# Cross-attention and mixture of experts on one core: key products in six banks, the maxima's scores of batch 0 ahead of most value products, normalisations and set-up transfers moved

## The reference, cut to what matters

```python
# x (8, 256, 256); ctx (8, 77, 256): 8 batches, 256 queries and 77 keys each, 16 heads of width 16
q1, q2 = heads(norm(x) @ q1_w.T), heads(norm(x) @ q2_w.T)
k1, v1 = heads(ctx @ kv1_w.T);  k2 = heads(ctx @ kv2_w.T)[keys]
attn = softmax(q1 @ k1.T / 4) - (lambda_1 - lambda_2 + 0.1) * softmax(q2 @ k2.T / 4)
x = x + rmsnorm(attn @ v1) * norm_w @ proj_w.T + proj_b
# then a mixture of 8 experts, two for each of the 2048 tokens
w, idx = top_k(softmax(norm(x) @ gate_w.T), 2);  w = w / sum(w)
x = x + sum over the two experts of w * (silu(g) * u) @ down.T,   g, u = norm(x) @ gate_up.T
```

## Time and profile before

| | |
|---|---|
| median of 3 runs | 556.19 us (552.88 to 559.12) |
| the profiled execution's own time | 557.22 us |
| its span, first to last instruction | 555.4 us |
| PE busy | 495.3 us (89%) |
| PEld busy | 363.6 us (65%) |
| VectorE busy | 386.1 us (70%) |
| ScalarE busy | 340.2 us (61%) |
| GpSimd busy | 273.4 us (49%) |
| granted TensorE clock, mean | 0.963 of full speed |
| chain that ended last | PE 67%, DVE 10%, ACT 7%, DMA 5% |

### The profile page before, as it was taken

The page is one execution under the profiler, slowest core; times in us unless marked ns, Lnnn a source line. Parts: engine busy times, 40 slices in busy tenths (PEclk is TensorE's granted clock), DMA queues, the critical chain, the costliest instruction groups (busy, mean ns, idle before and its releaser), DMA issues.

```text
span 555.4 us, 12114 instructions
## 1 busy us (share of the span) xinstructions
PE 495.3 (89%) x3741; PEld 363.6 (65%) x3756; DVE 386.1 (70%) x805; ACT 340.2 (61%) x642; POOL 273.4 (49%) x347
## 2 busy tenths in 40 slices
PE   4695889998999888799798999999999999999990
PEld 3463546775666555526566888878888888777750
DVE  5437458888888765788577997887667677666551
ACT  1220588888788888374675777766656566645530
POOL 5006464574564564203227566656567555644244
PEclk9986799999999989899999999999999999999996
DMA  7567757768658632563666777967555465554224
GB/s 215 191 171 174 239 147 231 203 171 264 192 170 253 200 118 76 179 204 112 152 137 111 158 129 195 180 120 157 94 104 86 85 84 101 96 68 77 30 30 47
DMA packets 88090, 79.89 MB, mean 144 GB/s; under 512 B 49176, under 2 KB 73368, under 8 KB 87896
## 3 DMA queue, kind: packets, MB, share of 16 engines
q1 hardware_dynamic: 76512, 63.38, 41.8%
q0 software_dynamic: 11520, 15.74, 17.6%
HBM read 49.08 MB, written 22.41 MB: 129 GB/s over the span
## 4 chain that ended last, share of the span: by engine, by line
PE 67%; DVE 10%; ACT 7%; DMA 5%; issue 5%; SPq 3%; POOL 2%; another core or an unknown queue 0%; ACTq 0%; POOLq 0%
PE bank L1459 27%; PE bank L1476 13%; PE bank L1242 5%; PE bank L1288 4%; DMA x_parts<-WE 3%; PE bank L1274 3%; PE bank L1488 2%; PE bank L1256 2%; PE bank L1311 2%; PE bank L1324 2%; DVE FB L1165 2%; PE bank L1297 2%; DVE FB L1169 2%; ACT FB L876 2%; PE bank L1336 2%
## 5 line engine op out<-in xcount | busy, mean ns | idle before, releaser
L1459 PE MATMUL bank<-FB,WE 128*128 128x0 bf16 x1440 | 187.6, 280 | 2.6 <-issue 1.0
L1459 PEld LDWEIGHTS bank<-FB,WE 128*128 x1440 | 136.1, 98 | 34.9 <-issue 4.3
L709 POOL DMA_INDIRECT out<-FB,slot_tok x60 | 99.9, 1665 | 91.2 <-DVE FB L1186 85.4
L876 ACT ACTIVATE FB<-FB 128x512 bf16<-128x512 f32 x120 | 75.6, 630 | 69.9 <-DVE FB L1165 63.8
L1169 DVE TENSOR_TENSOR FB<-FB 128x512 bf16<-128x512 f32 x120 | 83.3, 694 | 46.9 <-ACT FB L876 43.0
L1476 PE MATMUL bank<-FB,WE 128*128 128x0 bf16 x720 | 103.7, 280 | 4.3 <-DVE FB L1169 2.2
L1165 DVE TENSOR_TENSOR FB<-FB,bank 128x512 f32<-128x512 f32 x120 | 81.9, 683 | 27.8 <-ACT FB L870 21.5
L700 POOL DMA_INDIRECT FB<-x_parts,slot_tok x60 | 61.7, 1028 | 68.0 <-DMA FB<-FB 26.7
L870 ACT ACTIVATE FB<-bank 128x512 f32<-128x512 f32 x120 | 70.7, 589 | 33.9 <-PE bank L1459 29.3
L1476 PEld LDWEIGHTS bank<-FB,WE 128*128 x720 | 67.6, 98 | 23.5 <-issue 7.8
L633 POOL TENSOR_TENSOR WE<-FB,WE 128x256 bf16<-128x256 f32 x104 | 67.8, 678 | 22.1 <-ACT WE L740 22.0
(11 more groups left out here) (180 smaller groups left out, 616.4 us busy)
## 6 DMA issues: line engine op xcount, KB each, us to landing
FB<-w SPq DMA_DIRECT2D x26, 512.0 KB, 5.5
WE<-w SPq DMA_DIRECT2D x44, 256.0 KB
WE<-q_parts SPq DMA_DIRECT2D x32, 200.0 KB
WE<-x SPq DMA_DIRECT2D x16, 256.0 KB, 5.2
q_parts<-FB SPq DMA_DIRECT2D x32, 128.0 KB
x_parts<-WE SPq DMA_DIRECT2D x20, 128.0 KB, 4.0
out<-WE SPq DMA_DIRECT2D x20, 128.0 KB, 5.5
q_parts<-WE SPq DMA_DIRECT2D x16, 128.0 KB
```

Source lines behind the costliest of these rows:

```text
L709: pool.indirect_dma_start(out=out, out_offset=bass.IndirectOffsetOnAxis(ap=slot_tok[:, c:c + 1].bitcast(U32), axis=0), in_=result_tile(c), ...
L876: nc.scalar.activation(hT[k % 3][:, 0, :], hid[k % 2], ACT.Copy).then_inc(hi_ready, 1)
L1459: ins = nc.tensor.matmul(to, wf[:, bass.ds(at + o, P)], xgT[s % 2][:, 2 * part + kc, :].shape_from_register(long[s % 2]), start=(z == 0), ...
```

## The change

The keys of group m go to banks 2(m mod 3) and 2(m mod 3) + 1, so banks 0 to 5 hold them and group 3 reuses banks 0 and 1 after the first remainder. Values use banks 2 to 5 in turn. On PE the order becomes: keys, queries of batch 0, transpose of x of batch 1, values 0 and 1, queries of batch 1, scores groups 0 to 11 with values 2 to 5 after groups 1, 3, 5, 7 and the transpose of x of batch 2 after group 7; values 6 and 7 come after queries (1) of batch 2. VectorE's value copies move along, its statistics and norm of batch 1 go between the key remainders, the scaling of the projection weights comes before the values, the statistics of batch 2 between the two query remainders of batch 1 and its norm after the second maximum. On SyncE two of the eight pad transfers go between the keys' transfers, and the load of x of batch 2 goes ahead of the query transfers of batch 0. GpSimd's and ScalarE's lists stay as they are, but for the bank that `kh` reads.

```diff
--- before.py
+++ after.py
@@ -200,7 +200,7 @@
 
         banks = ctx.enter_context(nc.psum_tensor("bank", [P, 8, 512], F32))
         bank = [banks[:, i, :] for i in range(8)]
-        sc_bank, st_bank, v_bank, ot_bank = bank[0:2], bank[2:4], bank[4:6], bank[4]
+        sc_bank, st_bank, v_bank, ot_bank = bank[0:2], bank[2:4], bank[2:6], bank[4]
         A5, A6, A7 = bank[5], bank[6], bank[7]
         up_bank, turn_bank = [bank[0:2], bank[2:4]], bank[7]
         first_bank = bank[6], bank[7], bank[5], bank[0]
@@ -386,6 +386,10 @@
             for kind, n in end or ():
                 yield kind, n % TPB, n // TPB
 
+        def key_bank(m, n):
+
+            return 2 * (m % 3) + n
+
         def piece_of(b, w):
 
             n = SPLIT_FIRST + 3 * b + w
@@ -518,6 +522,11 @@
                 for a in range(2):
                     sp.dma_start(qst[b % 2][64 * a + 48:64 * a + 50, :, :], mT[2 * H * a:2 * H * (a + 1), :]).then_inc(m_in, 16)
 
+            def pads_of(i):
+                sp.wait_ge(zero_ready, 1)
+                sp.dma_start(xs[T + i * P:T + (i + 1) * P, :], o_sb[:, 0, :].bitcast(BF16)).then_inc(pads_out, 16)
+                sp.dma_start(out[T + i * P:T + (i + 1) * P, :], o_sb[:, 0, :]).then_inc(pads_out, 16)
+
             for n in range(STG):
                 load_piece(n)
             sp.wait_ge(stack0_ready, 1)
@@ -530,10 +539,12 @@
                 stack_out(kd, 0, kh, a, kd_out)
                 sp.wait_ge(kl_ready, 2 * a + 2)
                 stack_out(kd, 1, kl, a, kd_out)
+                if a == 0:
+                    pads_of(0)
+            load_x(2)
             for a in range(2):
                 queries_out(0, a)
                 queries_lo_out(0, a)
-            load_x(2)
             sp.wait_ge(kd_out, 16 * 4)
             sp.wait_ge(stack0_ready, 3)
             sp.wait_ge(zq_out, 64)
@@ -551,10 +562,8 @@
             for n in range(STG, SPLIT_FIRST + STG):
                 load_piece(n)
             load_x(3)
-            sp.wait_ge(zero_ready, 1)
-            for i in range(SUB):
-                sp.dma_start(xs[T + i * P:T + (i + 1) * P, :], o_sb[:, 0, :].bitcast(BF16)).then_inc(pads_out, 16)
-                sp.dma_start(out[T + i * P:T + (i + 1) * P, :], o_sb[:, 0, :]).then_inc(pads_out, 16)
+            for i in range(1, SUB):
+                pads_of(i)
             for kind, i, b in steps(SP_PLAN):
                 r = b * S + i * P
                 if kind == "QI":
@@ -801,7 +810,7 @@
                 act.wait_ge(kv_mm, m + 1)
                 for n in range(2):
                     w = B * SK // 2
-                    nc.scalar.activation(kh[:, m, n * w:(n + 1) * w], bank[2 * m + n][:, 0:w], ACT.Copy, scale=SCALE).then_inc(kh_ready, 1)
+                    nc.scalar.activation(kh[:, m, n * w:(n + 1) * w], bank[key_bank(m, n)][:, 0:w], ACT.Copy, scale=SCALE).then_inc(kh_ready, 1)
             for a in range(2):
                 q_hi(0, a)
             xnT_copy(1)
@@ -939,9 +948,13 @@
                 for n in range(2):
                     w = B * SK // 2
                     c = slice(n * w, (n + 1) * w)
-                    ins = nc.vector.scalar_tensor_tensor(out=kl[:, m, c], in0=bank[2 * m + n][:, 0:w], scalar=SCALE, in1=kh[:, m, c],
+                    ins = nc.vector.scalar_tensor_tensor(out=kl[:, m, c], in0=bank[key_bank(m, n)][:, 0:w], scalar=SCALE, in1=kh[:, m, c],
                                                          op0=ALU.mult, op1=ALU.subtract)
                 ins.then_inc(kl_ready, 1)
+                if m == 1:
+                    ln1_stats_of(1)
+                if m == 2:
+                    ln1_norm(1)
 
             def q_lo(b, a):
                 dve.wait_ge(qh_ready, 2 * b + a + 1)
@@ -967,25 +980,29 @@
                 nc.vector.scalar_tensor_tensor(out=lo, in0=src, scalar=-1.0, in1=hi,
                                                op0=ALU.mult, op1=ALU.subtract).then_inc(mneg_ready, 1)
 
+            def values_copy(b):
+                dve.wait_ge(v_mm, b + 1)
+                v = vp[0:SK, b, 0:H * VW].rearrange("p (h d) -> p h d", h=H)[:, :, 0:HD]
+                nc.vector.tensor_copy(v, v_bank[b % 4][0:SK, 0:D].rearrange("p (h d) -> p h d", h=H)).then_inc(v_ready, 1)
+
             q_lo(0, 0)
             q_lo(0, 1)
-            ln1_stats_of(1)
-            ln1_norm(1)
-            for b in range(B):
-                dve.wait_ge(v_mm, b + 1)
-                v = vp[0:SK, b, 0:H * VW].rearrange("p (h d) -> p h d", h=H)[:, :, 0:HD]
-                nc.vector.tensor_copy(v, v_bank[b % 2][0:SK, 0:D].rearrange("p (h d) -> p h d", h=H)).then_inc(v_ready, 1)
-            q_lo(1, 0)
-            q_lo(1, 1)
             dve.wait_ge(smalls_in, 16 * 9)
             for k in range(KC):
                 nc.vector.tensor_scalar(pj_sb[:, k, :], pj_sb[:, k, :], normw[:, k:k + 1], None, ALU.mult).then_inc(pj_ready, 1)
             step(nc.vector.tensor_tensor(lams[:, 2, :], lams[:, 1, :], lams[:, 0, :], ALU.subtract))
             step(nc.vector.tensor_scalar(lams[:, 2, :], lams[:, 2, :], -0.1, None, ALU.add))
+            for b in range(2):
+                values_copy(b)
+            q_lo(1, 0)
             ln1_stats_of(2)
-            ln1_norm(2)
+            q_lo(1, 1)
             for g in range(12):
                 maxima(0, g)
+                if g == 1:
+                    ln1_norm(2)
+                if g in (1, 3, 5, 7):
+                    values_copy(2 + g // 2)
             for kind, i, b in steps(DVE_PLAN, DVE_END):
                 n = TPB * b + i
                 if kind == "LS":
@@ -994,6 +1011,9 @@
                     ln1_norm(b)
                 if kind == "QL":
                     q_lo(b, i)
+                if (kind, i, b) == ("QL", 1, 2):
+                    values_copy(6)
+                    values_copy(7)
                 if kind == "MX":
                     maxima(b, i)
                 if kind == "NEG":
@@ -1318,31 +1338,39 @@
             w = B * SK // 2
             for m in range(4):
                 if m == 3:
-                    pe.wait_ge(xnT_ready, 1)
+                    pe.wait_ge(kl_ready, 1)
                 for n in range(2):
                     for k in range(KC):
-                        ins = nc.tensor.matmul(bank[2 * m + n][:, 0:w], wk_sb[:, k, m * P:(m + 1) * P], ctx_sb[:, k, n * w:(n + 1) * w],
+                        ins = nc.tensor.matmul(bank[key_bank(m, n)][:, 0:w], wk_sb[:, k, m * P:(m + 1) * P], ctx_sb[:, k, n * w:(n + 1) * w],
                                                start=(k == 0), stop=(k == KC - 1))
                 ins.then_inc(kv_mm, 1)
-            pe.wait_ge(kl_ready, 4)
+            def values(b):
+                if b == 0:
+                    pe.wait_ge(wv_in, 16 * KC)
+                if b < 4:
+                    pe.wait_ge(kl_ready, (2, 2, 3, 3)[b])
+                else:
+                    pe.wait_ge(v_ready, b - 3)
+                for k in range(KC):
+                    ins = nc.tensor.matmul(v_bank[b % 4][0:SK, 0:D], ctx_sb[:, k, b * SK:(b + 1) * SK], wv_sb[:, k, :],
+                                           start=(k == 0), stop=(k == KC - 1))
+                ins.then_inc(v_mm, 1)
+
             queries(0, 0)
             queries(0, 1)
             transposed_x(1)
-            pe.wait_ge(wv_in, 16 * KC)
-            for b in range(B):
-                if b - 1 > 0:
-                    pe.wait_ge(v_ready, b - 1)
-                for k in range(KC):
-                    ins = nc.tensor.matmul(v_bank[b % 2][0:SK, 0:D], ctx_sb[:, k, b * SK:(b + 1) * SK], wv_sb[:, k, :],
-                                           start=(k == 0), stop=(k == KC - 1))
-                ins.then_inc(v_mm, 1)
+            values(0)
+            values(1)
             queries(1, 0)
             queries(1, 1)
-            transposed_x(2)
             pe.wait_ge(pj_ready, 2)
             pe.wait_ge(smalls_in, 16 * 9)
             for g in range(12):
                 scores_for_max(0, g)
+                if g in (1, 3, 5, 7):
+                    values(2 + g // 2)
+                if g == 7:
+                    transposed_x(2)
             unit = [0]
 
             def differences(n):
@@ -1373,6 +1401,9 @@
                     transposed_x(b)
                 if kind == "Q":
                     queries(b, i)
+                if (kind, i, b) == ("Q", 1, 2):
+                    values(6)
+                    values(7)
                 if kind == "SC":
                     scores_for_max(b, i)
                 if kind == "MT":
```

## The result

The changed kernel takes 565.05 us in the median (563.99 to 566.98, 4 runs) against 556.25 (552.88 to 559.12) for the kernel before on the same chip: ratio 1.0164, 95% interval 1.0124 to 1.0204. It is slower, by 9 us. The forecast was 558.2 with a range of 551.0 to 563.0; the measured time lies 2 us outside. The profiled execution took 563.99 us with a span of 562.2, 6.8 longer than before. Where an execution ran slow as a whole (one of e4's four, 568.8 us), the ratio leaves it out and the median given does not.

What follows compares the result with a forecast made beforehand. PE was taken as the bound from 63.6 us on. First scores -4.5, GpSimd's wait +4.8 and low clock +1.7 summed to +2.0: profiled 559.2, median 558.2, range 551.0 to 563.0.

Steps and rivals of the forecast that it cites:

- The wait of 1.73: On PE, batch 0's queries would no longer wait 1.73 us for the last key remainder.
- the scores moved ahead: Batch 0's scores for the maxima on PE would begin some 14 us earlier and be done by 47.7.
- so the load is issued at 42.1: SyncE would issue the third weight piece's load at 42.1 in place of 49.32, giving transposed maxima at 53.0.
- the moved transfers: On SyncE, two pad transfers would cost nothing, at most 2.11 us uncovered; x of batch 2 loads before six query transfers.
- Behind it: constants 2.5; then low parts ... 7.0: On GpSimd, after the eighth value copy at 59.9, constants take 2.5 and low parts with roots 7.0, ending at 69.4.
- a lead of 7.2: Gain of 7.2 us up to batch 2's second query product on PE, before the last two values reduce it to 4.5.
- rival (d): First scores stay as now, GpSimd's wait moves the seventh group to 75.0: 563.7, median 562.7; chance 0.05.
- the clock: After PE's gap ahead of the seventh group, 3.4 us at half speed would cost 1.7 us.
- Rival (c): PE's clock stays low for 17 us after the gap at 65 to 70.5: 566.0, median 565; chance 0.12.
- no clock effect alone could make this kernel slower by over 1%: Limit on PE's clock cost, 5.6 us, read from the Trainium skill; the prediction said the rows don't bear it out.
- the landing of the piece: The third weight piece's load on SyncE would take 8.0 us to land, at 50.1.
- Rival (a): Same GpSimd wait, but clock stays up or the piece lands in 6.6 us: medians 555.1 to 556.8; chance 0.26.

Runs made afterwards that it cites:

- e4: The changed kernel with SyncE's pad transfers and load of x of batch 2 back at their old places: 562.8 us, ratio 1.0163.
- e1: The changed kernel with GpSimd's routing_constants called later, behind the second root for x of batch 4: 558.51 us, ratio 1.0049.
- e6: The changed kernel with e2's earlier values 6 and 7, e4's old SyncE places and e5's earlier loads of weight pieces 2 and 3: 551.83 us, ratio 0.9897.
- e2: The changed kernel with values 6 and 7 behind score groups 9 and 11 of batch 0: 556.33 us, ratio 1.0032.
- e3: The kernel before, with GpSimd's routing_constants also waiting for batch 1's first group of scores for the maxima: 560.76 us, ratio 1.0103.
- e5: The changed kernel with weight pieces 2 and 3 loaded on SyncE ahead of the fetch of batch 1's keys and queries: 563.71 us, ratio 1.0101.
- e8: The changed kernel with the edits of e2 and e4, so e6 without the early loads of weight pieces 2 and 3: 556.39 us, ratio 0.9966.
- e9: e6 with batch 0's shifts issued ahead of the eight pad transfers and x of batch 3 loaded ahead of weight pieces 2 and 3: 549.96 us, ratio 0.9817.

## Why the prediction was wrong

**Right: what the change wins.** The wait of 1.73 went, the scores moved ahead (to 36.2, where I had 32.5), and their end at 47.7 does not matter, because the third piece lands ten microseconds after it.

**Wrong: "so the load is issued at 42.1".** This is the step that failed. It was issued at 50.22, and 7.3 us that I booked as won never were: the transposed maxima came at 60.3, not 53.0. The sum behind 42.1 took three durations from the earlier trace rows that the changed kernel does not keep. (1) The fetch of batch 0's queries: 28.4 predicted, 31.73 measured. The last query part started at 26.41, not 24.8, as the issues ahead of it stretched (2.34 for two where the rows had 1.18), and it was awaited 5.3 us, not 3.6. (2) Batch 1's query parts out: from the first issue at 36.29 to the last at 42.33, 6.0 in place of 3.1. (3) Their landing, from 42.33 to 47.8, 5.5 in place of 3.6. Together 3.3 + 2.9 + 1.9 = 8.1, which is the miss.

A part of (1) is a term that I put at nothing: the moved transfers. I let the pads hide in SyncE's wait for ScalarE, and gave the load of x of batch 2 no price at all. ScalarE's first query copy ended at 19.50, but SyncE issued that part at 21.53, 2.0 later; in e4, without the moved transfers, it went out at 19.68, right behind a copy that ended at 19.66. The table under e4 puts them at some 2.7 by the fetch. That the fetch was late by 3.3 only is luck in part: the copy itself started at 18.90, where my sum has 20.9 (22.60 in the kernel before, less 1.73), and in e1 and e6 it started at 20.50 and 21.29.

The rest is crowding, by argument and not by a run of its own. In the kernel before each batch's query parts went out on a quiet queue: 4.7 us lie between the last key copy's issue at 34.37 + 1.21 and batch 1's parts at 40.24. The changed kernel has no such wait. I took durations from a stretch with gaps and used them for a stretch without.

**Right, and the reason for the loss: GpSimd's queue.** "Behind it: constants 2.5; then low parts ... 7.0": from the eighth copy at 66.6 to the last root at 76.0 it took 9.4, where I had 9.5, and the seventh group came 10.5 after the copy, where I had 10.6. The gap was 5.90, where I had 5.4. e1, e2 and e3 each show that it is this wait. By my sum a lead of 7.2 would have been cancelled by it (no run has that lead together with the wait: e5 comes nearest); with none it is a plain loss. I had worked that case out as rival (d), at 562.7, and gave it 0.05 with the words that nothing shows a landing that long. No single landing had to be long: three moderate delays in a row did it. The measured time lies above (d) too: (d) has the first scores where they were and 1.7 for the clock, and by the rows they came 2.0 later with 2.8 for the clock.

**Too small: the clock.** I took 1.7, for 3.4 us at the low clock. The low stretch behind the gap was 7.6 us in the changed kernel and 5.8 in e3, and cost 2.8 (9.7 less 6.9) and 2.2 (6.3 less 4.1). The stretch without gaps that I counted on did come, with PE busy 7.60 of 7.60 us and 5.80 of 5.80, but the clock stayed at 0.50 for longer than the 3.4 us of the earlier trace rows; why, the runs do not show. The cost is less than half of the length, where I had taken half. Rival (c), 17 us, did not come either. The Trainium skill (TensorE: Matmul & The Clock Gate, section on the HAM clock gate) holds the ramp under 1% of a typical span, and the 2.8 us after this one gap are 0.5% of it, which agrees in size. The page says it of a kernel's first matmuls, not of stretches behind gaps further on, and this kernel has more than one stretch at 0.50 (50.6 to 60.3 and 74.5 to 84.7 in the windows above), so my step from it to "no clock effect alone could make this kernel slower by over 1%" did not follow.

**Right: the landing of the piece.** It took 7.7 (50.22 to 57.91); I had 8.0. Rival (a), a landing of 6.6, did not come.

By the rows the sum is: first scores +2.0 (I had -4.5), gap beyond that +4.9 (+4.8), clock +2.8 (+1.7), 9.7 at batch 1. The span ends only 6.8 later; 1.6 of the difference is back by the first expert product and 1.3 after it. Which waits gave it back I have not followed; the medians differ by 8.8, and the profiled execution is the shortest of the changed kernel's four, so a part of it may be no more than the spread between executions.

## What to carry to other kernels

When work is moved later, look in every queue, the unedited ones above all, for waits on it: here a wait that was free in one order stood ahead of the next stage's pace-setter in the other. When work is moved closer together, the durations and landings of its transfers do not move with it; price them from the busiest row, not from the one with the same name. And before a stage is pulled forward, find what the stage behind it waits for: once the values stood early and the transfers at their old places (e8, no difference from before that can be told), e6 and e9 moved loads and two shifts in SyncE's list, at no cost in work, and these two are faster than the kernel before.

## What the runs showed of the hardware

The issue of a transfer is not a fixed cost. Over the first 75 us a query part (128 KB) took 0.57 us to issue in the median and 0.735 at most in the kernel before (1.28 at most in the whole of it), and up to 1.88 in the changed one; a pad transfer, 0.43 at least, took 2.13 at 16.59, behind two key copies and another pad. SyncE was held in the issue itself, not in a wait on a semaphore, and whatever stood behind it in its list was late too. Whether a full queue holds the issue or the transfer engines' speed does, these runs do not tell apart: e4, with two pads and one load of x taken out of the way, still shows 2.57 and 3.63 for a pair of issues.
